# A selective state scan recast: time on the partitions, running sums as TensorE products

## The reference

```python
dlt = softplus(dlt)                                        # B, K, E, L
dA = dlt[..., None] * A_log[None, :, :, None, :]           # B, K, E, L, N
phi = exp(-cumsum(dA, axis=3))                             # over time
dbx = dlt[..., None] * swapaxes(b, 2, 3)[:, :, None] * xs[..., None]
h = phi * cumsum(dbx / (phi + 1e-12), axis=3)
y = einsum('bkdln,bknl->bkdl', h, c) + Ds[None, :, :, None]
```

## Time and profile before

| | |
|---|---|
| median of three runs | 2948.95 us (lowest 2946.0) |
| span of the profiled execution | 2938.3 us |
| what lies around the span (median less span) | 10.65 us |
| busy: PE / DVE / ACT / POOL | 2263.7 / 2503.6 / 1743.5 / 1896.0 us |
| `l0_steps`, read from the trace | 101.2 to 280.6 us |
| `l0_scan`, read from the trace | 280.6 to about 1985 us |
| all that follows | 1985 to 2938.3 us |

### The profile page before, as it was taken

How to read it: one execution, slowest core, us unless ns; L and a number is a source line. 1 busy time by engine, 2 the same in 40 slices (tenths; PEclk the granted TensorE clock), 3 DMA queues, 4 the chain that set the end, 5 groups by cost and what they waited for, 6 DMA issues and landing times. The chain is left out here.

```text
span 2938.3 us, 27688 instructions
## 1 busy us (share of the span) xinstructions
PE 2263.7 (77%) x8714; PEld 1197.9 (41%) x8714; DVE 2503.6 (85%) x2085; ACT 1743.5 (59%) x2935; POOL 1896.0 (65%) x646
## 2 busy tenths in 40 slices
PE   6853677777877777787777778778984999799579
PEld 3421234343443434343443434444442555355444
DVE  5657999999999999999999999986787777699721
ACT  1566787878888888888878788863230000263220
POOL 0166999999999999999999999984000000198000
PEclk9967799999999999999999999998997999899689
DMA  1277445555454555545455554535005453100360
GB/s 48 88 219 272 102 112 137 130 124 130 115 133 118 131 136 123 129 112 132 119 131 134 125 129 112 135 90 191 0 0 143 110 129 104 43 8 8 82 89 24
DMA packets 145457, 323.07 MB, mean 110 GB/s; under 512 B 48219, under 2 KB 63840, under 8 KB 140320
## 3 DMA queue, kind: packets, MB, share of 16 engines
q1 hardware_dynamic: 144224, 317.17, 42.7%
q10 hardware_dynamic: 1088, 4.13, 0.6%
HBM read 234.46 MB, written 46.87 MB: 96 GB/s over the span
## 5 line engine op out<-in xcount | busy, mean ns | idle before, releaser
L903 POOL TENSOR_TENSOR l0c_r<-l0c_r,l0c_v 128x1536 f32<-128x1536 f32 x253 | 869.4, 3442 | 96.3 <-DVE l0c_r L862 96.3
L940 ACT ACTIVATE ps<-l0c_dlt,l0c_na 128x512 f32<-128x512 f32 (+1 forms) x1152 | 625.5, 574 | 286.5 <-DVE l0c_h L891 267.2
L912 POOL TENSOR_TENSOR l0c_hcp<-l0c_cb,l0c_h 128x1536 f32<-128x1536 f32 x216 | 743.2, 3446 | 5.5 <-DVE l0c_h L891 4.1
L891 DVE TENSOR_TENSOR_SCAN l0c_h<-ps,l0c_h,l0c_r 128x768 f32<-128x768 f32 x384 | 694.1, 1808 | 1.8 <-issue 1.2
L818 PE MATMUL ps<-l0c_hcp,net_ident 128*128 128x512 f32 x1728 | 645.2, 496 | 25.2 <-ACT l_Z L933 11.9
L950 ACT ACTIVATE l0c_r<-l0c_S,l0c_floor,l0c_na 128x768 f32<-128x768 f32 x576 | 579.9, 1014 | 0.1
L862 DVE SCALAR_TENSOR_TENSOR l0c_r<-l0c_r,ps 128x768 f32<-128x768 f32 x576 | 536.1, 931 | 18.1 <-issue 8.5
L752 PE MATMUL ps<-l0c_Bp,l0c_sel 96*128 96x512 bf16 x1012 | 256.0, 335 | 301.1 <-DVE l0c_hcv L869 146.1
L818 PEld LDWEIGHTS ps<-l0c_hcp,net_ident 128*128 128x128 f32 x1728 | 299.2, 193 | 297.6 <-issue 216.9
L891 DVE TENSOR_TENSOR_SCAN l0c_h<-ps,l0c_r 128x768 f32<-128x768 f32 x192 | 335.4, 1747 | 0.0
L1628 PE MATMUL ps<-l_prod,l_wa 128*96 128x384 f32 (+1 forms) x888 | 292.1, 493 | 25.7 <-DVE l_prod L1545 25.7
(11 more groups left out here) (280 smaller groups left out, 2739.9 us busy)
## 6 DMA issues: line engine op xcount, KB each, us to landing
l0c_cb<-cf SPq DMA_DIRECT2D x432, 384.0 KB, 5.5
l_other<-l_p SPq DMA_DIRECT2D x22, 864.0 KB, 6.0
dlt<-l0s_dl SPq DMA_DIRECT2D x36, 384.0 KB, 2.3
v<-l0s_vv SPq DMA_DIRECT2D x36, 384.0 KB, 2.9
l0c_dlt<-dlt SPq DMA_DIRECT2D x36, 384.0 KB, 3.6
l0c_v<-v SPq DMA_DIRECT2D x36, 384.0 KB, 4.4
l_other<-l_p SPq DMA_DIRECT2D x22, 288.0 KB, 6.7
l0c_Bp<-bc SPq DMA_DIRECT2D x36, 144.0 KB, 3.8
```

What stands on the lines that cost most here:

```text
L891: dve.tensor_tensor_scan(h[:, n, :], da[j % 2], r[:, j % NR, :], init, ALU.mult, ALU.add).then_inc(s_scan, 1)
L903: pool.tensor_tensor(two, two, v[:, (j // N) % 2, :].unsqueeze(1).to_broadcast([128, 2, SEG]), ALU.mult).then_inc(s_w, 2)
L912: pool.tensor_tensor(hcp[:, p % NHP:p % NHP + 2, :], cb[:, p % NCB:p % NCB + 2, :], h[:, e % N:e % N + 2, :], ALU.mult).then_inc(s_hp, 2)
L940: act.activation(da[e % 2][:, part], dlt[:, i, part], ACT.Exp, scale=na[:, i, n:n + 1]).then_inc(done, 1)
```

## The change: what it does

`l0_scan` is written anew. A unit is now one chunk of SPAN = 127 time steps x 128 rows x all 16 states. There are NCH = 19 chunks for each direction (the last has 18 steps), so U = 4 x 19 x 3 = 228 units. Time lies on the partitions and (state, row) along the free axis, 2048 columns wide:

- `exponents` (PE): the running sum S of dlt (128 rows x 127 times, as weights) times `Ad`, a 128 x 2048 image with A_log on its diagonals, gives S * A for all states: four products of 512 columns.
- `decay`, Ln and `inverse` (ACT): phi = Exp(-S A), then Ln(phi + 1e-12) and Exp of its negative, three passes over 2048 columns. Ln works on phi * 2^-24, and b and c are stored times 2^-12.
- `turned_v` (PE): v turned by a product with the identity.
- `inputs` (DVE): v times the inverse, two halves of 1024 columns.
- `sums` (PE): for every state, a triangular 127 x 128 image `TB` that holds b (weights) times the inputs gives the running sum over time. Row 127 of the inputs is the carry from the chunk before, brought by a DMA from row 127 of `ph`, and column 127 of TB yields the next carry. For tiles 0 and 2 that is 16 products of 128 columns, for tile 1 (two images, so two b's) 32 of 64 columns.
- `decayed` (DVE): times phi, two halves.
- `outputs` (PE): for every state, h (weights) times a diagonal image `DC` that holds c, added over the states in PSUM: 16 products of 127 columns, or for tile 1 32, each with 64 weight columns, to partitions 0 to 63 and 64 to 127 in turn.
- `gather` (DVE): 127 columns added into the result.
- POOL makes TB and DC with `affine_select`, 127 x 16 x 127, one of each for every chunk and image.

`l0_steps` now also takes the running sum of dlt along time (a DVE scan, L527 of the changed kernel) and stores S in place of dlt. It makes b and c with time on the partitions: 72 chunks x 3 products whose weights are 127 columns of x and whose moving operand is 64 columns, in twelve batches of 18, and a last batch of 12 for the chunks of 18 steps. The bf16 parts, the copies of c and their stores are gone. All products of the new scan are f32.

```diff
 # l0_scan, PE
+            def exponents(u):
+                pe.wait_ge(s_ld[u % NL], 32 * (u // NL + 1))
+                pe.wait_ge(s_ad[t], 16 * (i + 1))
+                if u:
+                    pe.wait_ge(s_phi, u)
+                for q in range(4):
+                    mm = pe.matmul(ps[:, PSA + BANK * q:PSA + BANK * (q + 1)], Sc[:, u % NL, :],
+                                   Ad[:, t, BANK * q:BANK * (q + 1)], start=True, stop=True)
+                mm.then_inc(s_sa, 1)
+            def turned_v(u):
+                if u:
+                    pe.wait_ge(s_w, 2 * u)
+                pe.matmul(ps[0:SPAN, PV:PV + 128], vc[:, u % NL, 0:SPAN], ident[:, :], start=True, stop=True
+                          ).then_inc(s_vt, 1)
+            def sums(u, half):
+                m = matrix(u, image(u, half))
+                pe.wait_ge(s_tb, 2 * m + 2)
+                pe.wait_ge(s_w, 2 * u + half + 1)
+                pe.wait_ge(s_carry[u % NBUF], 16 * (u // NBUF + 1))
+                if u or half:
+                    pe.wait_ge(s_h, 2 * u + half)
+                for n in states(u, half):
+                    cols = columns(u, half, n)
+                    at = PCUM + cols.start - half * HALF
+                    mm = pe.matmul(ps[:, at:at + cols.stop - cols.start], TB[:, m % NBUF, n, :], qw[:, u % NBUF, cols],
+                                   start=True, stop=True)
+                mm.then_inc(s_cum, 1)
+            def outputs(u):
+                pe.wait_ge(s_h, 2 * u + 2)
+                if u:
+                    pe.wait_ge(s_out, u)
...
+            for u in range(U):
+                sums(u, 0)
+                if u:
+                    outputs(u - 1)
+                if u + 1 < U:
+                    turned_v(u + 1)
+                sums(u, 1)
+                if u + 2 < U:
+                    exponents(u + 2)
 # ACT
+            def decay(u):
+                act.wait_ge(s_sa, u + 1)
+                if u >= NBUF:
+                    act.wait_ge(s_y, u - NBUF + 1)
+                    act.wait_ge(s_carry[u % NBUF], 16 * (u // NBUF + 1))
+                act.activation(ph[:, u % NBUF, :], ps[:, PSA:PSA + WIDE], ACT.Exp, scale=-1.0).then_inc(s_phi, 1)
+            def inverse(u):
+                act.wait_ge(s_ln, u + 1)
+                qu = qw[0:SPAN, u % NBUF, :]
+                act.activation(qu, qu, ACT.Exp, scale=-1.0).then_inc(s_q, 1)
+            for u in range(U + 1):
+                if u < U:
+                    decay(u)
+                if u:
+                    inverse(u - 1)
+                if u < U:
...
+                    act.activation(qw[0:SPAN, u % NBUF, :], ph[0:SPAN, u % NBUF, :], ACT.Ln, bias=eps[0:SPAN, :],
+                                   scale=2.0 ** -24).then_inc(s_ln, 1)
 # DVE
+            for u in range(U + 1):
+                if u < U:
+                    inputs(u, 0)
+                if u >= 2:
+                    gather(u - 2)
+                if u:
+                    decayed(u - 1, 1)
+                if u < U:
+                    inputs(u, 1)
+                    decayed(u, 0)
 # SP, for every unit
+                    sp.wait_ge(s_h, 2 * (u - NBUF + 1))
+                    src = ph[SPAN:SPAN + 1, (u - T) % NBUF, :]
+                sp.dma_start(qw[SPAN:SPAN + 1, u % NBUF, :], src).then_inc(s_carry[u % NBUF], 16)
+                if u + 2 < U:
+                    chunk_load(u + 2)
 # POOL, for every chunk and image
+                    pool.affine_select(TB[0:SPAN, m % NBUF, :, 0:SPAN], spread(k, j, b, 0), [[0, N], [sign, SPAN]],
+                                       ALU.is_ge, zero, base=0, channel_multiplier=-sign).then_inc(s_tb, 1)
...
+                    pool.affine_select(DC[0:SPAN, m % NBUF, :, 0:SPAN], spread(k, j, b, 1), [[0, N], [1, SPAN]],
+                                       ALU.is_equal, zero, base=0, channel_multiplier=-1).then_inc(s_dc, 1)
```

More of the change, by code:

```diff
@@ L372, in part_rows @@
[L372 to L381, removed]
+            sp.dma_start(d["z"], Z[:, 0:T, :]).then_inc(s_out, 16)
@@ new lines, in l0_scan @@
+        s_ld = [sem(f"ld{i}") for i in range(NL)]
+        s_carry = [sem(f"carry{i}") for i in range(NBUF)]
+        s_sa, s_vt, s_cum, s_y = map(sem, "sa vt cum y".split())
+        s_phi, s_ln, s_q = map(sem, "phi ln q".split())
+        s_w, s_h, s_out = map(sem, "w h out".split())
+        s_tb, s_dc = map(sem, "tb dc".split())
+        block = ctx.enter_context(nc.Block())
+        U = K * NCH * T
+        PSA, PCUM, PV, PY = 0, 4 * BANK, 6 * BANK, 7 * BANK
+        def place(u):
+            c, t = divmod(u, T)
+            i, j = divmod(c, NCH)
+            k = UNITS[i]
+            return i, k, NCH - 1 - j if k % 2 else j, t
@@ new lines, in first_chunk, with size, image, matrix @@
+        def first_chunk(u):
+            return u // T % NCH == 0
+        def size(u):
+            return REST if place(u)[2] == NCH - 1 else SPAN
+        def image(u, half):
+            t = place(u)[3]
+            return half if t == 1 else t // 2
+        def matrix(u, b):
+            return u // T * B + b
+        def states(u, half):
+            return range(N) if place(u)[3] == 1 else range(half * N // 2, (half + 1) * N // 2)
+        def columns(u, half, n):
+            return slice(half * HALF + 64 * n, half * HALF + 64 * n + 64) if place(u)[3] == 1 else \
+                slice(128 * n, 128 * n + 128)
@@ L746, in _ @@
+            for i in range(NL):
+                sp.wait_ge(s_ld[i], 32 * len(range(i, U, NL)))
+            for i in range(NBUF):
+                sp.wait_ge(s_carry[i], 16 * len(range(i, U, NBUF)))
         @block.tensor
         def _(pe):
[L748 to L754 removed]
@@ L825, in _ @@
[L825 to L835 removed]
+            def exponents(u):
+                i, k, j, t = place(u)
+                pe.wait_ge(s_ld[u % NL], 32 * (u // NL + 1))
[6 more added lines that the diff above has]
+                mm.then_inc(s_sa, 1)
@@ new lines, in decayed, with gather @@
+            def decayed(u, half):
+                dve.wait_ge(s_cum, 2 * u + half + 1)
+                pu = ph[:, u % NBUF, half * HALF:(half + 1) * HALF]
+                dve.tensor_tensor(pu, ps[:, PCUM:PCUM + HALF], pu, ALU.mult).then_inc(s_h, 1)
+            def gather(u):
+                i, k, j, t = place(u)
+                m = size(u)
+                if i == 2 and first_chunk(u):
+                    dve.wait_ge(s_dsum, 1)
+                    dve.wait_ge(s_out, u)
+                    dve.tensor_scalar(by_image(Y[:, t, :]), Y[:, t + 1, :].rearrange("p (w h) -> p h w", h=H),
+                                      dsum[:, t:t + 1], None, ALU.add).then_inc(s_dsum, 1)
+                    dve.wait_ge(s_dsum, t + 2)
+                dve.wait_ge(s_y, u + 1)
+                to = Y[:, t + 1 if i < 2 else t, SPAN * j:SPAN * j + m]
+                if i:
+                    dve.wait_ge(s_out, u - T + 1)
+                    dve.tensor_tensor(to, to, ps[:, PY:PY + m], ALU.add).then_inc(s_out, 1)
+                else:
+                    dve.tensor_copy(to, ps[:, PY:PY + m]).then_inc(s_out, 1)
```

664 lines of the change are left out of this document (212 added, 452 removed).

## The result

The changed kernel takes 6221.25 us (median of 4 runs, 6219.67 to 6222.17), against 2950.4 us before, the median of 4 runs. One of these took 7862.56 us and the others 2946.0 to 2951.9; without that slow run the changed kernel takes 2.111 times the time, with an interval of 2.108 to 2.114. The profiled execution has a span of 6219.8 us. The forecast was 6270 us, slower.

What follows compares the result with a forecast made beforehand. The prediction took PE's work, the waits behind it and its lowered clock to bound the scan: 12.4 + 6.9 + 2.5 = 21.8 us for each of 228 units, 4970 us; with the other stages 6270 us, range 5550 to 7050.

Steps and rivals of the forecast that it cites:

- the queue of waits: In each scan unit, PE idles while ACT and DVE instructions run one behind the other: 6.9 us (6.4 to 7.4).
- the clock: In each scan unit, PE runs at half speed for some 5.1 us after its gap, losing 2.5 us (0 to 3.4).
- PE's work: PE's products in a mean scan unit over the three tiles: 12.4 us (10.8 to 13.8).
- the five durations: Within PE's wait: `decay` 1.84, `inverse` 1.88, `inputs` 1.22, `gather` 0.28 and `decayed` 1.22 us.
- the hand-overs of 0.05: Within PE's wait in each scan unit: five passes from one instruction to the next, 0.05 us each.
- The 10.65 us: Added to the summed 6262.5 us of the profiled execution, as the amount by which the median stands above the span.
- cheap end of all its terms: Low case of the range: a scan unit of 10.8 + 6.4 + 1.7 = 18.9 us, `l0_steps` at 190, so 5580 us.
- `l0_steps`: This stage grows from 179.4 to 218 us (190 to 260), through DVE's running sum and PE's b and c products.
- Units that overlap: Rival: neighbouring scan units slide over each other, so a unit is PE's 12.4 us; 4130 us, chance 0.05.
- POOL as the bound: Rival: POOL's selects limit the scan from 16 us a select; at 25 us, 8900 us; chance 0.07.
- PE at the low level throughout: Rival: PE's clock stays low through the scan and its work doubles; 8530 us, chance 0.06.
- Faster through cheap small products: Rival: TensorE takes small f32 products side by side and ACT's 5.6 us a unit become the limit; 2600 us, chance 0.01.

Runs made afterwards that it cites:

- run 1: The changed kernel with ACT issuing `inverse` of the unit before ahead of the next `decay`: 4051.68 us, a unit 12.06 us.
- run 4: The changed kernel with 25 unused identity products added on PE in each unit's gap behind the exponents: 5594.06 us.
- run 3: The changed kernel with ACT's `inverse` ahead of `decay` and DVE's `decayed` ahead of `inputs`: 4051.95 us.
- run 7: The changed kernel with each GpSimd select issued four times in a row: 6223.39 us.
- run 9: The changed kernel with ACT's and DVE's reorderings, bfloat16 products (lower precision) and the exponents in two halves: 2805.52 us, 0.952 of the time before.
- run 5: The changed kernel with only the first 15 of 25 unused identity products added on PE in each unit's gap: 6047.97 us.
- run 2: The changed kernel with DVE's second-half `decayed` of the unit before ahead of `inputs` and `gather`: 5957.5 us, a unit 20.43 us.

## Why the prediction was right, step by step

- **The path.** PE, then the queue of waits, then the clock: the mechanism was right, and runs 1 and 4 show its parts. With the queue removed a unit is PE's work alone (run 1); with the queue left and the clock held up it is 18.83 us (run 4), where 12.06 and 6.61 make 18.67.
- **PE's work**, forecast 12.4 us, measured 12.06. I took 0.118 us for an instruction on the full tiles; at full clock 16 of them start 1.95 - 0.17 us before the next group, so 0.111, the lower end from the earlier trace rows. The middle tile's sums cost 0.110, forecast 0.10. The 0.107 by columns of weights, which the prediction took from the Trainium skill (TensorE: Matmul & The Clock Gate, "LDWEIGHTS"), was the better guide here. It holds at the high clock only: at a granted clock of 0.50 the same 32 instructions took 7.06 us, 0.215 each. The middle tile's outputs cost (3.69 - 0.17) / 64 = 0.055, forecast 0.07: such products do overlap in pairs, better than in the earlier trace rows. So the sums of this tile were 0.6 us dearer than forecast and its outputs 1.0 cheaper, and the two misses partly cancel.
- **The queue of waits**, forecast 6.9 us with PE's tail, measured 6.44 + 0.17 = 6.6. Each of the five durations was right within 0.05 us; the hand-overs of 0.05 were in part already in them, since one instruction often starts before the one ahead is recorded as ended (2041.28 + 1.88 = 2043.16, and L773 starts at 2043.05).
- **The clock**, forecast 2.5 us, measured 2.76 by run 4. From the unit itself, 21.59 - 12.06 - 6.61 = 2.9. The basis was thinner than the prediction says. Of the two gaps that it names, only the one before 163 shows a fall: the granted clock is 1.00 from 157 to 160, 0.76 from 160 to 163 and then 0.50. Ahead of the 6.0 us without work the level had been 0.50 since 171.7, so that row shows a low level that lasted through a gap and not one that a gap brought.
- **The sum.** A unit is 21.59 in place of 21.8, since two terms were 0.3 too large and one 0.3 to 0.4 too small. That the total came within 1% is in part luck: the misses have different signs. 228 x 0.21 = 48 us less; the first fill (23.7 in place of 20) and the stages behind the scan add some 5, which leaves the 43 us between 6262.5 and the span of 6219.8. The 10.65 us that were added to the span are not there: the median stands 1.5 us above it, and in all runs whose own span is on record, the kernel before among them, the time is 1.7 to 1.9 us above it (once 2.65). The 10.65 came from setting a median beside the span of another, quicker execution. The range has a slip too: its "cheap end of all its terms" takes 1.7 us for the clock, where the term itself says 0. With 0 a unit would be 17.2 us and the cheap end about 5200 us.
- **`l0_steps`**, forecast 218 us, measured 217.2. The 36 products for b and c, 72 instructions, take 8.09 us (7.2 forecast) in a unit of 9.27 (9.5). That the unit agrees is luck in part: an instruction cost 0.11 and not 0.10 us, and the two waits for ACT that the forecast added do not show, since PE goes from one group to the next without a gap:

```profile
130.40 8.09 PE L398 MATMUL ps<-l0e_w_bc,l0e_XI 128*127 128x64 f32 x72
...
138.32 1.51 PE L426 MATMUL ps<-l0s_P,l0e_w_up 128*128 128x512 f32 x4
...
139.67 8.09 PE L398 MATMUL ps<-l0e_w_bc,l0e_XI 128*127 128x64 f32 x72
```

- **What was to be seen.** PE busy for 3464 / 228 = 15.2 us a unit (14 to 15), ACT 1269 us in the scan (1280), DVE 1124 (1180), the gap ended by L807, the clock 0.81: right or nearly so. POOL was busy for 653 us, under the 700 to 1400: a select of 2032 columns takes 2.03 us, 1.00 ns a column, just under the lower bound of 2.2 that I drew from a one-input product.
- **The rivals.** Units that overlap, priced at 4130 us with a chance of 0.05: the order doesn't let them, but it was one instruction away, and then took 4052. The price was right. Of the three reasons that stood against it, ACT's order was the one that counted: DVE's order was worth nothing once ACT's was changed (run 3), and the single set of banks for the exponents left PE busy throughout (run 1). POOL as the bound: excluded by run 7 up to four times its work. PE at the low level throughout: no, it comes back in each unit. Faster through cheap small products: false for float32. With bfloat16, another order and the exponents in two halves the kernel is 5% faster than before (run 9), though the limit then was not ACT's work alone.

What is not settled: why gaps with the same 3.15 us of idle time lower the clock in some units and not in others (run 5), and what holds the last kernel at 6.59 us.

## What to carry to other kernels

When a step moves to another engine, write down each engine's list of instructions for one round and look for the last wait in each, before counting busy time: here one ACT instruction that stood behind a wait it didn't need cost 2170 us, more than float32 products instead of bfloat16 ones. Many small float32 products are priced by their instructions (two each, 0.11 us with 128 weights, at 64 columns as at 128), so up to that width count instructions and not columns; at 512 columns an instruction took (3.60 - 0.17) / 8 = 0.43 us. A gap on PE can cost more than its length: 6.6 us of waits came to 9.53 with the clock, and in run 2 a gap that was shortened by 1.37 us gave back 1.16.
